# Mirrored image rows folded around the column transform, with plain fp32 matmuls in array halves

## Chip, cores and metric

One core of a Trainium2 chip runs the whole program in one launch. The metric is device time in microseconds (us), the median of several executions.

## What is computed

The reference is a network of a convolutional mixer, linear attention and a small feed-forward block on eight images of 56x56 positions with 256 channels. The change touches the mixer: a long two-dimensional convolution, done as a Fourier transform over image columns and rows, a product with the transform of a generated kernel, and the transform back. Cut to that part:

```python
xn = simple_rms(x)
u = jax.nn.silu(xn @ W_u.T + b_u)          # 8 x 56 x 56 x 512, the gate
v = jax.nn.silu(xn @ W_v.T + b_v)          # 8 x 56 x 56 x 512
g = rpe_coeffs(...)                        # 111 x 111 taps for each channel
y = irfft2(rfft2(v) * rfft2(g))[:56, :56]  # along both image axes, each channel by itself
out = (u * y) @ W_o.T + b_o + x
```

Everything is fp32. The kernel transforms with matmuls by cosine and sine matrices of 111 points, in place of a fast transform.

## The kernel before

The program runs its phases one after the other: `kernel_rows_phase` makes the taps and transforms them along rows; `project_phase` (names pr_) computes v and its row transform; `columns_phase` (co_) does the column transform, the product and the column transform back; `mix_phase` (mx_) does the row transform back, the gate and the output product; attention and feed-forward follow. Between phases the data lie in device memory (`v_rows`, `y_rows`). Each engine's program is an order written out by hand; engines meet at counting semaphores, and each queue (PE, DVE, ACT, POOL, and SP, which issues DMAs) is strictly in order.

**Project phase.** 56 chunks of 8 image rows, 4 tiles each (two image rows at partitions 0 to 55 and 64 to 119). For a chunk PE transposes x (L1064), projects four tiles (L135, three fp32r passes for each product), and makes the row transform of each tile as two fp32 matmuls, one for each half of the array's rows (L1084). DVE adds the bias (L1220), ACT applies silu (`gate`, L1142), and ACT and DVE copy the results out (L1148, L1228). POOL normalises x four chunks ahead (`normalise`, L1047 and L1051). SP, for chunk n, issues the load of x for chunk n+4 and then waits for chunk n's rows to store them: so the load for n+4 stands behind the store of chunk n-1.

**Column phase.** 56 frequencies (k), each with the spectrum of the taps and eight images (b). v is stacked to 112 partitions, its real and imaginary part. ACT and DVE split v and the taps into a high and a low fp32r part (L837, L882, L841, L887). PE makes, for an image, six fp32r matmuls forward (L135, `forward`) and two fp32 matmuls back (L806, L808, `inverse`), and twelve fp32r matmuls for the next frequency's spectrum. DVE multiplies with the spectrum (L902, L904), POOL adds the terms (L925, L928), and ACT copies the result (L862) and, in one go of three, the spectrum (L846). PE runs the inverse of an image two images behind its forward (`LAG = 2`); two PSUM slots hold forward results.

**Mix phase.** 56 chunks again: PE makes the row transform back (L1485) as two fp32 matmuls, one for each half of the array's columns, DVE multiplies it by the gate straight from PSUM (`mix`, L1710), PE turns and multiplies by W_o. POOL does two normalise and two residual operations for a chunk (L1429, L1433, L1442, L1445).

The order of a frequency on PE before:

```python
for b in range(LAG, BATCH):
    if b == BATCH // 2 + 1 and more:
        spectrum(k + 1)
    forward(k, b)
    inverse(k, b - LAG)
for b in range(LAG):
    if more:
        forward(k + 1, b)
    inverse(k, BATCH - LAG + b)
```

## Time and profile before

| | |
|---|---|
| median of three executions | 5406.36 us (5403.94 to 5410.94) |
| profiled execution, first to last instruction (span) | 5398.1 us |
| busy share of the span | PE 97%, PE's weight loads 68%, DVE 74%, ACT 47%, POOL 46% |
| project phase, 56 chunks | from about 677 to 1271 us |
| column phase, 56 frequencies | from about 1299 to 2847 us |
| mix phase, 56 chunks | from about 2858 to 3907 us |

The profiled execution's own device time is not listed apart from the three; 8.3 us of the median lie outside its span. In the timeline a row gives start and duration of one instruction or of several of the same kind in a row, and in brackets how long its engine had been idle and what released it. A matmul's duration holds its fill and drain, so the spacing of starts tells what it costs PE in a stream.

### The profile page before, as it was taken

What the parts mean: (1) busy time and instruction counts of PE and PEld (TensorE: products, weight loads), DVE (VectorE), ACT (ScalarE), POOL (GpSimd) and SP (SyncE); (2) the same over time, 40 slices, a digit from 0 to 9 for tenths busy, and PEclk for the clock granted to TensorE, in tenths of its full rate; (3) what the DMA queues carried; (4) which work ended last, traced back from release to release, by engine and by line L of the source; (5) the groups of instructions that cost most, each with busy time, mean ns of one, the idle gap of its engine ahead of it and who ended that gap; (6) DMA issues with size and microseconds to landing.
All of it is one profiled execution on the core that took longest, in us unless ns stands there. A gap on an engine that the chain in (4) does not pass through costs nothing. (4 is left out here: it accounts for less than half of the span.)

```text
span 5398.1 us, 89326 instructions
## 1 busy us (share of the span) xinstructions
PE 5214.1 (97%) x27048; PEld 3662.3 (68%) x27048; DVE 3997.7 (74%) x6176; ACT 2512.3 (47%) x4791; POOL 2489.9 (46%) x1381
## 2 busy tenths in 40 slices
PE   8999899997999999999998999999989999987999
PEld 6777655554555555555556777777767777765999
DVE  6777666666999999999996676766635666665887
ACT  5555577774434334343434555555532222211555
POOL 0000054443999999999995555555301111111332
PEclk9999999998999999999999999999999999998999
DMA  3222167775444444444446666666533333433443
GB/s 109 89 89 72 53 197 219 217 217 170 149 150 150 149 152 148 152 148 150 151 136 182 195 203 200 191 200 202 163 113 97 104 113 107 118 89 97 123 122 113
DMA packets 349121, 782.62 MB, mean 145 GB/s; under 512 B 43433, under 2 KB 147845, under 8 KB 339460
## 3 DMA queue, kind: packets, MB, share of 16 engines
q1 hardware_dynamic: 326596, 703.91, 44.2%
q10 hardware_dynamic: 22400, 77.08, 4.0%
q8 instruction: 73, 1.20, 0.1%
q14 instruction: 52, 0.43, 0.0%
HBM read 420.49 MB, written 360.38 MB: 145 GB/s over the span
## 5 line engine op out<-in xcount | busy, mean ns | idle before, releaser
L928 POOL TENSOR_TENSOR co_prod<-co_cross 111x512 f32<-111x512 f32 x448 | 848.8, 1895 | 0.0
L862 ACT ACTIVATE co_y_out<-co_y_ps 112x512 f32<-112x512 f32 x448 | 267.9, 598 | 928.2 <-PE co_y_ps L808 923.1
L925 POOL TENSOR_TENSOR co_prod<-co_direct 111x512 f32<-111x512 f32 x448 | 576.3, 1286 | 203.8 <-PE co_y_ps L808 116.0
L902 DVE TENSOR_TENSOR co_direct<-co_v_ps,co_spec 111x1024 f32<-111x1024 f32 x448 | 543.5, 1213 | 92.0 <-PE co_v_ps L135 87.9
L2012 POOL TENSOR_TENSOR at_t<-at_t,at_p_bias 112x1024 f32<-112x1024 f32 x56 | 137.7, 2470 | 889.3 <-DMA at_t<-t_tiles 889.3
L904 DVE TENSOR_TENSOR co_cross<-co_v_ps,co_spec 111x1024 f32<-111x1024 f32 x448 | 541.5, 1209 | 0.0
L135 PE MATMUL co_v_ps<-co_v_high,co_col_fwd_high 112*111 112x512 f32 x896 | 506.1, 565 | 1.4 <-DVE co_cross L904 1.4
L806 PE MATMUL co_y_ps<-co_prod,co_col_inv 111*112 111x512 f32 x896 | 458.2, 592 | 0.0
L808 PE MATMUL co_y_ps<-co_prod,co_col_inv 111*112 111x512 f32 x896 | 457.5, 592 | 0.1
L882 DVE TENSOR_TENSOR co_v_low<-co_v_in,co_v_high 112x1024 fp32r<-112x1024 f32 x224 | 372.3, 1662 | 0.0
L135 PE MATMUL co_v_ps<-co_v_low,co_col_fwd_high 112*111 112x512 f32 x896 | 354.3, 395 | 0.0
L2173 ACT ACTIVATE at_qk_t<-at_bank_ps 128x448 f32<-128x448 f32 x224 | 121.6, 543 | 499.1 <-PE at_bank_ps L135 499.1
L135 PE MATMUL co_v_ps<-co_v_high,co_col_fwd_low 112*111 112x512 f32 x896 | 349.1, 390 | 0.0
L1596 ACT ACTIVATE mx_mixed_high<-mx_turn_ps 128x448 fp32r<-128x448 f32 x224 | 121.8, 544 | 431.1 <-PE mx_turn_ps L1495 431.1
L808 PEld LDWEIGHTS co_y_ps<-co_prod,co_col_inv 111*112 111x112 f32 x896 | 156.0, 175 | 229.3 <-issue 212.3
L1220 DVE SCALAR_TENSOR_TENSOR pr_v_pre<-pr_v_ps,pr_inv,pr_v_bias 120x512 f32<-120x512 f32 x224 | 167.6, 748 | 150.8 <-PE pr_v_ps L135 145.5
L1442 POOL TENSOR_TENSOR mx_resid<-mx_x_in,mx_o_bias 112x1024 f32<-112x1024 f32 x56 | 134.0, 2393 | 311.2 <-DVE mx_t L1726 311.2
L306 POOL CAST kr_points<-kr_coords 6x448 fp32r<-6x448 f32 x28 | 15.2, 568 | 565.8 <-DMA kr_coords<-coords 565.8
L2502 POOL TENSOR_TENSOR ff_base<-ff_t,ff_n 112x1024 f32<-112x1024 f32 x56 | 132.7, 2370 | 301.3 <-DVE ff_out L2663 281.5
L1047 POOL TENSOR_TENSOR pr_gx<-pr_x_in,gn_rows 128x1024 f32<-128x1024 f32 x55 | 133.0, 2419 | 298.1 <-DMA pr_x_in<-x 298.1
L135 PE MATMUL mx_o_ps<-mx_w_o_high,mx_mixed_high 128*112 128x256 f32 x896 | 252.3, 282 | 3.5 <-DVE mx_mixed_low L1715 3.5
L135 PE MATMUL mx_o_ps<-mx_w_o_high,mx_mixed_low 128*112 128x256 f32 x896 | 252.2, 281 | 0.0
(277 smaller groups left out, 14268.5 us busy)
## 6 DMA issues: line engine op xcount, KB each, us to landing
v_rows<-pr_rows_out SPq DMA_DIRECT2D x56, 1792.0 KB, 8.2
co_v_in<-v_rows SPq DMA_DIRECT2D x448, 224.0 KB
y_rows<-co_y_out SPq DMA_DIRECT2D x448, 224.0 KB
mx_y_in<-y_rows SPq DMA_DIRECT2D x224, 448.0 KB, 5.5
kr_x_in<-x SPq DMA_DIRECT2D x56, 448.0 KB, 3.9
kern_rows<-kr_rows_out SPq DMA_DIRECT2D x28, 896.0 KB, 4.7
pr_x_in<-x SPq DMA_DIRECT2D x112, 224.0 KB
mx_x_in<-x SPq DMA_DIRECT2D x56, 448.0 KB, 5.3
```

What stands on the lines that cost most here:

```text
L135: last = nc.tensor.matmul(out, weights[a], data[b], start=start and i == 0, stop=stop and i == len(passes) - 1)
L806: nc.tensor.matmul(y_ps[b % 2][:2 * SIDE, :], col_inv[:, 0, :], prod[b % 2][:, :WIDE], start=True, stop=False)
L808: nc.tensor.matmul(y_ps[b % 2][:2 * SIDE, :], col_inv[:, 1, :], prod[b % 2][:, WIDE:], start=False, stop=True).then_inc(inv_mm, 1)
L862: nc.scalar.activation(y_out[:, b, :], y_ps[b % 2][:2 * SIDE, :], ACT.Copy).then_inc(y_ready, 1)
L882: nc.vector.tensor_tensor(v[1][:, images, :], v_in[:, images, :], v[0][:, images, :].bitcast(F32), ALU.subtract).then_inc(low_v, 1)
L902: nc.vector.tensor_tensor(direct[b % 2][:], v_ps[b % 2][:POINTS, :], spec[i][:, :2 * WIDE], ALU.mult).then_inc(real_terms, 1)
L904: nc.vector.tensor_tensor(cross[b % 2][:], v_ps[b % 2][:POINTS, :], spec[i][:, WIDE:], ALU.mult).then_inc(multiplied, 1)
L925: nc.gpsimd.tensor_tensor(prod[b % 2][:, :WIDE], direct[b % 2][:, :WIDE], direct[b % 2][:, WIDE:], ALU.subtract).then_inc(real_ready, 1)
L928: nc.gpsimd.tensor_tensor(prod[b % 2][:, WIDE:], cross[b % 2][:, :WIDE], cross[b % 2][:, WIDE:], ALU.add).then_inc(combined, 1)
L1220: nc.vector.scalar_tensor_tensor(out=v_pre[t % 2][:], in0=v_ps[t % 2][:SPAN, :], scalar=inv[:SPAN, j % GROUP * TILES + t:j % GROUP * TILES ...
L1442: nc.gpsimd.tensor_tensor(resid[u][:], x_in[u][:], o_bias[:].unsqueeze(1).to_broadcast(each), ALU.add).then_inc(resid_part, 1)
L2012: nc.gpsimd.tensor_tensor(t1[j % HELD][:], t1[j % HELD][:], p_bias[:].unsqueeze(1).to_broadcast([TILE, TILES, CH]), ALU.add).then_inc(t1_b ...
```

## The change

The image rows are stored in mirrored pairs (by the caller, outside the kernel, and put back there): each group of four is two rows and their mirror images. In the project phase POOL adds (`add_rows`) and DVE subtracts (`subtract_rows`) two tiles of silu results into `fold`, and the row transform takes `fold`. The even and odd parts that result make the column transform of an image real: two fp32 matmuls with 56 input rows each, in the two halves of the array's rows, and back two fp32 matmuls with 56 outputs each, in the two halves of its columns. No fp32r splits are left in the column phase. DVE writes all four terms of the product in one operation of 2048 elements; POOL adds them for six images of eight in one operation of 1024, and for images 2 and 6 PE adds them, with four matmuls. The inverse runs three images behind. The spectrum is four full fp32 matmuls, spread over four images, and its four copies on ACT are spread over images 4 to 7. In the mix phase ACT copies the odd part out of PSUM (`take_odd`), DVE unfolds (`unfold`), and POOL, in place of DVE, multiplies by the gate.

```diff
@@ columns_phase, PE
+                def spectrum(k, out, part):
...
+                    last = nc.tensor.matmul(taps_ps[:POINTS, bass.ts(out, WIDE)], col_taps[:, matrix, :], taps_in[:, part, :],
+                                            start=part == 0, stop=part == 1)
...
                 def forward(k, b):
                     n = k * BATCH + b
-                    pe.wait_ge(low_v, k * PAIRS + b // 2 + 1)
-                    buffer_free(pe, multiplied, n)
-                    for out in range(2):
-                        last = product(nc, v_ps[b % 2][:POINTS, bass.ts(out, WIDE)], [w[:, out, :] for w in col_fwd],
-                                       [x[:, b, :] for x in v], start=True, stop=True)
+                    pe.wait_ge(v_loaded[b // 2], k * 32 + 32)
+                    wait_slot(pe, multiplied, n)
+                    for part in range(2):
+                        side = slice(part * GAP, part * GAP + SIDE)
+                        last = nc.tensor.matmul(v_ps[b % 2][:POINTS, bass.ts(part, WIDE)], col_fwd[side, :], v_in[side, b, :],
+                                                start=True, stop=True)
...
+                    if b in SUMMED_BY_PE:
+                        pe.wait_ge(multiplied, SLOTS + n + 1)
+                        for term in range(2):
+                            for part in range(2):
+                                last = nc.tensor.matmul(y_ps[b % 2][part * GAP:part * GAP + SIDE, :],
+                                                        col_inv[:, part * SIDE:(part + 1) * SIDE],
+                                                        terms[b % RING][:, bass.ts(2 * part + term, WIDE)],
+                                                        start=term == 0, stop=term == 1)
...
                     for b in range(LAG, BATCH):
-                        if b == BATCH // 2 + 1 and more:
-                            spectrum(k + 1)
+                        if more and b > LAG:
+                            spectrum(k + 1, *divmod(b - LAG - 1, 2))
                         forward(k, b)
                         inverse(k, b - LAG)
@@ columns_phase, ACT (after the change; SUMMED_BY_PE = (2, 6), LAG = 3, TERMS = 4)
+                        if more and b >= TERMS:
+                            spectrum(k + 1, 1 - i, b - TERMS)
+                        wait_inverse(act, k, b)
...
+                    if col == TERMS - 1:
+                        last.then_inc(spec_ready, 1)
@@ columns_phase, DVE
                     dve.wait_ge(spec_ready, k + 1)
                     for b in range(BATCH):
...
+                        twice = [POINTS, 2, 2 * WIDE]
+                        nc.vector.tensor_tensor(terms[b % RING][:].rearrange("p (t n) -> p t n", t=2),
+                                                v_ps[b % 2][:POINTS, :].unsqueeze(1).to_broadcast(twice),
+                                                spec[i][:].rearrange("p (t n) -> p t n", t=2), ALU.mult).then_inc(multiplied, 1)
@@ project_phase, POOL
-                for n in range(1, GROUPS * GROUP):
-                    normalise(n // GROUP, n % GROUP)
+                def add_rows(s, j, pair):
+                    n = (s * GROUP + j) * PAIRS + pair
+                    done(pool, v_ready, 2 * n + 1)
+                    fold_free(pool, s, j, 2 * pair)
+                    nc.gpsimd.tensor_tensor(fold[2 * pair][:], v[2 * pair][:], v[2 * pair + 1][:], ALU.add).then_inc(sums_ready, 1)
...
+                for n in range(last + 1):
+                    add_rows(n // GROUP, n % GROUP, 1)
+                    if n + GROUP <= last:
+                        normalise((n + GROUP) // GROUP, n % GROUP)
+                    if n < last:
+                        add_rows((n + 1) // GROUP, (n + 1) % GROUP, 0)
@@ project_phase, PE
                 def row_pass(s, j, t):
                     n = (s * GROUP + j) * TILES + t
-                    done(pe, v_ready, n)
+                    pe.wait_ge(diffs_ready if t % 2 else sums_ready, (s * GROUP + j) * PAIRS + t // 2 + 1)
@@ mix_phase, POOL
+                for g in range(2 * PAIRS):
+                    mix(g, 0)
+                    mix(g, 1)
+                    if g + 2 < 2 * PAIRS:
+                        normalise((g + 2) // 2, g % 2)
+                    mix(g, 2)
+                    mix(g, 3)
+                    if g + 1 < 2 * PAIRS:
+                        residual((g + 1) // 2, (g + 1) % 2, first=g == 0)
@@ mix_phase, DVE
+                def unfold(s, u, pair):
+                    n = (s * 2 + u) * (TILES // 2) + pair
+                    dve.wait_ge(odd_ready, n + 1)
+                    for t, op in ((2 * pair, ALU.add), (2 * pair + 1, ALU.subtract)):
+                        once_past(dve, turned, (s * 2 + u - 1) * TILES + t + 1)
+                        nc.vector.tensor_tensor(gated[t][:], y_ps[0][:SPAN, :], odd[pair][:], op).then_inc(unfolded, 1)
```

Line numbers below are those of the changed kernel: L814 is the forward matmul, L832 and L825 the inverse (L825 where PE adds the terms), L803 the spectrum; L866 copies the spectrum and L878 a result on ACT; L1053, L1057 and L1063 are POOL's normalise and `add_rows`.

PE in the column phase, in the next to last frequency of the changed kernel, from the third piece of the next spectrum on:

```order
L803 MATMUL co_taps_ps<-co_taps_in,co_col_taps 111x512
L814 MATMUL co_v0_ps<-co_v_in,co_col_fwd 111x512 x2
L832 MATMUL co_y1_ps<-co_prod3,co_col_inv 56x512 x2
L803 MATMUL co_taps_ps<-co_taps_in,co_col_taps 111x512
L814 MATMUL co_v1_ps<-co_v_in,co_col_fwd 111x512 x2
L832 MATMUL co_y0_ps<-co_prod0,co_col_inv 56x512 x2
L814 MATMUL co_v0_ps<-co_v_in,co_col_fwd 111x512 x2
L832 MATMUL co_y1_ps<-co_prod1,co_col_inv 56x512 x2
L814 MATMUL co_v1_ps<-co_v_in,co_col_fwd 111x512 x2
L825 MATMUL co_y0_ps<-co_terms2,co_col_inv 56x512 x4
L814 MATMUL co_v0_ps<-co_v_in,co_col_fwd 111x512 x2
```

The seventh row is the forward matmul of the next frequency's image 0, the ninth that of its image 1, and the last that of its image 2; the tenth is the inverse of image 6. Between forward and inverse PE goes from row halves to column halves for every image, and the spectrum's pieces use the full array.

ACT in the same place, from image 3's copy of the result on:

```order
L878 ACTIVATE co_y_out<-co_y1_ps 120x512
L866 ACTIVATE co_spec1<-co_taps_ps 111x512
L878 ACTIVATE co_y_out<-co_y0_ps 120x512
L866 ACTIVATE co_spec1<-co_taps_ps 111x512
L878 ACTIVATE co_y_out<-co_y1_ps 120x512
L866 ACTIVATE co_spec1<-co_taps_ps 111x512
L878 ACTIVATE co_y_out<-co_y0_ps 120x512
L866 ACTIVATE co_spec1<-co_taps_ps 111x512
L878 ACTIVATE co_y_out<-co_y1_ps 120x512
```

The fourth copy of the spectrum, which releases the next frequency on DVE, now stands behind the result of image 6; before, three copies stood together ahead of the result of image 4.

POOL in the project phase, of the changed kernel, over one chunk and a half:

```order
L1053 TENSOR_TENSOR pr_gx0<-pr_x_in0,gn_rows 128x1024
L1057 TENSOR_TENSOR pr_gx0<-pr_gx0,gn_rows 128x1024
L1063 TENSOR_TENSOR pr_fold0<-pr_v0,pr_v1 120x512
L1063 TENSOR_TENSOR pr_fold2<-pr_v2,pr_v3 120x512
L1053 TENSOR_TENSOR pr_gx1<-pr_x_in1,gn_rows 128x1024
L1057 TENSOR_TENSOR pr_gx1<-pr_gx1,gn_rows 128x1024
L1063 TENSOR_TENSOR pr_fold0<-pr_v0,pr_v1 120x512
```

And before:

```order
L1047 TENSOR_TENSOR pr_gx0<-pr_x_in0,gn_rows 128x1024
L1051 TENSOR_TENSOR pr_gx0<-pr_gx0,gn_rows 128x1024
L1047 TENSOR_TENSOR pr_gx1<-pr_x_in1,gn_rows 128x1024
L1051 TENSOR_TENSOR pr_gx1<-pr_gx1,gn_rows 128x1024
L1047 TENSOR_TENSOR pr_gx2<-pr_x_in2,gn_rows 128x1024
```

The sum of tiles 0 and 1 of the next chunk, on which its first row transform waits, now stands behind the normalising of the chunk four ahead, which waits for the load of x. SP's order is as it was.

## Rows read from the trace of the kernel before

**Rows 1.** Windows: steady project, column, mix phase; length, busy: PE, PEld, DVE, ACT, POOL.

```profile
697.00:1267.00 570.00, 570.00 (x2605) 338.96 (x2603) 373.34 (x596) 450.18 (x1043) 244.85 (x103) 1.00 0.70 216
1326.00:2820.00 1494.00, 1494.00 (x4991) 870.84 (x4990) 1409.12 (x1140) 596.45 (x870) 1362.90 (x870) 1.00 0.49 149
2885.00:3890.00 1005.00, 1005.00 (x6496) 769.72 (x6495) 699.07 (x1459) 568.12 (x966) 513.57 (x216) 1.00 0.66 194
```

**Rows 2.** Timeline of PE in the column phase: start, duration, line.

```profile
2033.46 0.59 PE L806 MATMUL co_y_ps<-co_prod,co_col_inv 111*112 111x512 f32 x1
2033.89 1.02 PE L808 MATMUL co_y_ps<-co_prod,co_col_inv 111*112 111x512 f32 x2
2034.35 0.79 PE L135 MATMUL co_taps_ps<-co_taps_high,co_col_taps_high 111*111 111x512 f32 x1
2034.98 0.40 PE L135 MATMUL co_taps_ps<-co_taps_low,co_col_taps_high 111*111 111x512 f32 x1
2035.21 0.39 PE L135 MATMUL co_taps_ps<-co_taps_high,co_col_taps_low 111*111 111x512 f32 x1
...
2061.89 0.79 PE L135 MATMUL co_taps_ps<-co_taps_high,co_col_taps_high 111*111 111x512 f32 x1
```

**Rows 3.** Timeline of PE in the project phase, into and out of row halves.

```profile
1004.71 0.40 PE L135 MATMUL pr_v_ps<-pr_w_v_high,pr_x_t_low 128*120 128x512 f32 x1
1005.03 1.97 PE L1084 MATMUL pr_row_ps<-pr_v,pr_row_fwd 56*112 56x512 f32 x8
1006.94 0.50 PE L135 MATMUL pr_v_ps<-pr_w_v_high,pr_x_t_high 128*120 128x512 f32 x1
1007.27 0.39 PE L135 MATMUL pr_v_ps<-pr_w_v_low,pr_x_t_high 128*120 128x512 f32 x1
```

**Rows 4.** Timeline of PE in the mix phase, into and out of column halves.

```profile
3302.36 0.55 PE L1514 MATMUL mx_turn_ps<-mx_ident,mx_n 112*128 112x112 f32 x4
3302.84 1.93 PE L1485 MATMUL mx_y_ps<-mx_y_in,mx_row_inv 112*56 112x512 f32 x8
...
3305.03 0.39 PE L135 MATMUL mx_u_ps<-mx_w_u_low,mx_x_t_high 128*120 128x512 f32 x1
```

**Rows 5.** Timeline of DVE, then POOL, in the column phase.

```profile
2002.15 1.21 DVE L904 TENSOR_TENSOR co_cross<-co_v_ps,co_spec 111x1024 f32<-111x1024 f32 x1
2003.29 1.39 DVE L882 TENSOR_TENSOR co_v_low<-co_v_in,co_v_high 112x1024 fp32r<-112x1024 f32 x1
...
2003.54 2.29 POOL L928 TENSOR_TENSOR co_prod<-co_cross 111x512 f32<-111x512 f32 x1
...
2007.11 1.30 POOL L928 TENSOR_TENSOR co_prod<-co_cross 111x512 f32<-111x512 f32 x1
```

**Rows 6.** Timeline of ACT in the column phase; the first row follows PE L808.

```profile
2013.30 0.60 ACT L862 ACTIVATE co_y_out<-co_y_ps 112x512 f32<-112x512 f32 x1 [5.29 <-PE co_y_ps L808]
2013.79 1.56 ACT L846 ACTIVATE co_spec<-co_taps_ps 111x512 f32<-111x512 f32 x3
```

**Rows 7.** Attention phase: timeline of PE, then windows (third last column: clock).

```profile
3971.29 0.21 PE L2042 MATMUL at_bank_ps<-at_total_eps,at_row_head 128*32 128x1 f32 x5 [3.35 <-DVE at_sel L2255]
...
3972.00:3973.00 1.00, 1.00 (x9) 0.27 (x5) 0.00 (x0) 0.00 (x0) 0.00 (x0) 0.50 0.67 251
...
3975.00:3976.00 1.00, 1.00 (x12) 0.39 (x8) 0.00 (x0) 0.00 (x0) 0.04 (x1) 0.82 1.06 315
```

**Rows 8.** Timeline of SP, then POOL, then PE, in the project phase.

```profile
1012.96 0.36 SPq L1004 DMA_DIRECT2D v_rows<-pr_rows_out  x1
1013.58 2.09 SPq L999 DMA_DIRECT2D pr_x_in<-x  x2
...
1022.80 2.42 POOL L1047 TENSOR_TENSOR pr_gx<-pr_x_in,gn_rows 128x1024 f32<-128x1024 f32 x1 [5.49 <-DMA pr_x_in<-x]
1025.31 2.38 POOL L1051 TENSOR_TENSOR pr_gx<-pr_gx,gn_rows 128x1024 f32<-128x1024 f32 x1
...
1026.05 1.54 PE L1084 MATMUL pr_row_ps<-pr_v,pr_row_fwd 56*112 56x512 f32 x5
```

More of the change, by code:

```diff
@@ L60, in angles, with mirrored_rows, folded_slots @@
     return 2.0 * np.pi * ((np.outer(a, b) % POINTS) / POINTS)
+HALF_ROWS = CHUNK_ROWS // 2
+def mirrored_rows():
+    order = []
+    for first in range(0, SIDE // 2, 2):
+        order += [first, first + 1, SIDE - 1 - first, SIDE - 2 - first]
+    return np.array(order)
+def folded_slots():
+    place = np.arange(SIDE)
+    return place // CHUNK_ROWS * HALF_ROWS + place % HALF_ROWS, place % CHUNK_ROWS >= HALF_ROWS
 def shape_constants():
@@ L718, in pair_ahead, with wait_pooled, wait_inverse @@
-        def pair_ahead(k, b, more, ahead):
-            pair = b // 2 + ahead
-            if b % 2 == 0 and pair < PAIRS:
-                return k, pair
-            return (k + 1, pair - PAIRS) if b % 2 == 0 and more else None
+        def wait_pooled(eng, k, b):
+            if b >= 0:
+                eng.wait_ge(combined, (k + 1) * len(POOLED) + POOLED.index(b) + 1)
+            else:
+                eng.wait_ge(combined, k * len(POOLED) + POOLED.index(b + BATCH) + 1)
+        def wait_inverse(eng, k, b):
+            eng.wait_ge(inv_mm, (k + 1) * BATCH + b + 1)
@@ L821, in step @@
                         inverse(k, BATCH - LAG + b)
-                pe.sem_inc(inv_mm, SLOTS)
-                spectrum(0)
+                pe.sem_inc(inv_mm, BATCH)
+                pe.wait_ge(consts_in, 16 * len(loads))
+                for piece in range(4):
+                    spectrum(0, *divmod(piece, 2))
+                pe.wait_ge(y_clear, SLOTS)
                 for b in range(LAG):
@@ L868, in _ @@
-                split_taps(0)
-                for pair in range(HIGH_AHEAD):
-                    split_v(0, pair)
-                spectrum(0, 0)
+                for col in range(TERMS):
+                    spectrum(0, 0, col)
                 with act.Fori(0, LOOP) as s:
@@ L991, in columns, with slot, fold_free @@
             return slice(j % GROUP * TILES, (j % GROUP + width) * TILES)
+        PAIRS = TILES // 2
+        def slot(t, r):
+            return t % 2 * HALF_ROWS + t // 2 * 2 + r
+        def fold_free(eng, s, j, t):
+            if not (isinstance(s, int) and s == 0 and j == 0):
+                eng.wait_ge(row_mm, (s * GROUP + j - 1) * TILES + t + 1)
         with nc.Block() as block:
@@ L1083, in row_pass @@
                         side = slice(r * GAP, r * GAP + SIDE)
-                        last = nc.tensor.matmul(row_ps[t % 2][r][:ROWS, :], row_fwd[side, :], v[t][side, :], start=True, stop=True)
+                        last = nc.tensor.matmul(row_ps[t % 2][r][:ROWS, :], row_fwd[side, t % 2, :], fold[t][side, :],
+                                                start=True, stop=True)
                     last.then_inc(row_mm, 1)
@@ L1666, in step @@
                         store_t1(*before)
+                    if after:
+                        open_gate(*after, 1)
                     if later:
@@ L1776, in step @@
                     if now:
-                        low_part_mixed(*now, 0)
-                        mix(*now, 1)
+                        unfold(*now, 1)
+                        low_part_mixed(*now, 1)
+                    if before:
+                        residual(*before, 1)
                     if before2:
@@ L1782, in step @@
                         scale_gate(*after, 0)
-                    if before:
-                        residual(*before, 1)
                     if now:
-                        low_part_mixed(*now, 1)
-                        mix(*now, 2)
+                        low_part_mixed(*now, 2)
                     if before3:
                         take_norm(*before3)
-                    if after:
-                        scale_gate(*after, 1)
                     if before:
```

345 lines of the change are left out of this document (161 added, 184 removed).

## Prediction

> **What bounds the kernel now.** I first took the busy time of each engine over three steady stretches, since a total says nothing of stages [rows 1]. The first number after the length is PE's: it is busy for 570.0 us of 570, 1494.0 of 1494 and 1005.0 of 1005, at full clock. So in all three phases PE's own work sets the time, and the next engines are below it: in the column phase DVE with 1409 of 1494 and POOL with 1363. A change there pays only if it takes time from PE and no wait takes its place. Second, the timeline of PE, for the price of a matmul. In a stream an fp32 matmul of 512 columns comes as two passes whose starts lie 0.43 apart (2033.46, 2033.89), so 0.86 for one; an fp32r pass takes 0.23 (2034.98 to 2035.21) [rows 2]. A frequency lasts 2061.89 - 2034.35 = 27.54 us; 60 fp32r passes at 0.23 and 16 fp32 matmuls at 0.86 make 27.56. The model of PE closes. Third, the timelines of the other queues, for durations and for what each waits for.
>
> **Column phase: PE's work.** Two matmuls in opposite halves of the array already run side by side: eight passes in row halves issue in 1.7 us [rows 3], as do eight in column halves [rows 4], so four half matmuls cost what two full ones do. A frequency of the new kernel has 8 forward pairs, 6 inverse pairs, 2 images with two inverse pairs each, and 4 full matmuls of the spectrum: 22 x 0.86 = 18.9 us.
>
> Each change between full array and halves costs something. In the project phase the last full pass begins at 1004.71 and takes 0.23, the next full pass after the row halves ends its 0.23 before 1007.27; between lie 1007.04 - 1004.94 = 2.10 us for passes worth 4 x 0.43 = 1.71, so 0.39 for two changes [rows 3]. For column halves: four turns of 0.095 from 3302.36 end at 3302.74, the next full pass begins at 3305.03 - 0.23 = 3304.80, so 2.06 - 1.71 = 0.35 for two [rows 4]. I take 0.18 for one. The order has 20 changes in a frequency, 8 between full array and halves and 12 straight from row halves to column halves or back. No row shows a straight one. Its bounds are 0, if both halves count as one mode, and 0.37, if it is a way out and a way in; I take 0.18, nearest to both measured kinds. One change falls into the wait below, so 19 x 0.18 = 3.4 us.
>
> The Trainium skill, TensorEngine Tiling (Array Packing), section Tiling Modes, says that changing the tiling mode, and not just the tile, drains TensorE. By that rule, which speaks against this change, the straight changes are paid in full; without it they would be free and a frequency 12 x 0.18 = 2.2 us shorter, 121 us over the phase.
>
> **Column phase: a new wait.** At each frequency's start DVE's product for image 0 waits for the fourth copy of the spectrum. On ACT that copy stands behind the result of image 6, whose inverse on PE comes right before the forward of the next frequency's image 2; and this forward needs the slot that the product of image 0 frees. So from the issue's end of inverse 6: 0.16 until the last matmul is out (0.59 long, 0.43 apart [rows 2]), 0.49 for the result's copy and 0.60 for the spectrum's (0.60 long, next one 0.49 later [rows 6]), the product of 2048 elements, and four handovers of 0.04 to 0.05. A product of 1024 elements takes 1.21, and DVE's next operation starts 1.14 after it [rows 5], so one of 2048 takes at most 1.14 + 1.21 = 2.35 and, with one fixed part less, about 2.3. Sum: 3.7 us in which PE has nothing. DVE's 8 x 2.3 = 18.4 us and POOL's 6 x 2.4 = 14.4 (2.38 for 1024 elements [rows 8]) fit in the frequency, so nothing else waits. Frequency: 18.9 + 3.4 + 3.7 = 26.0 us.
>
> But such a gap moves the clock. After PE had stood idle for 3.35 us its granted clock went from 1.00 to 0.50 in the window at 3972, and the one at 3975 is back to 0.82 [rows 7]: some 3.4 us at 1.2 GHz in place of 2.4, so up to 1.7 us lost. The new gap is longer than that one. Part of the slow stretch falls on handovers, so I take 1.35: 27.4 us against 27.54, 56 x -0.14 = **-8 us**. The first frequency's preparation has no splits left, four of 512 elements at some 0.7 us (a little over half of 1.21): **-3**.
>
> **Project phase: the decisive part.** PE's matmuls stay the same in number and price. DVE gains two subtractions of 512 elements (some 0.7 each) on top of 373/570 x 10.51 = 6.9 us for a chunk, POOL two additions of 1.30 (a 512-element operation, the second POOL row of [rows 5]) on top of 4.9; neither fills 10.51 us. But the row transform now waits for POOL, and POOL's order puts normalise(n+4) ahead of the addition for tiles 0 and 1 of chunk n+1. Normalise waits for its x: the last rows show POOL idle 5.49 us before it, released by the DMA [rows 8]. SP, in an unchanged order, issues that load behind the store of chunk n-1. So a loop closes: the row transform of chunk n-1 begins at 1005.03 [rows 3], its rows are stored at 1012.96, the load goes out at 1013.58 and lands at 1022.80, 17.77 after the start; normalise ends 2.5 + 2.4 later, at 22.7; the addition takes 1.30 and some 0.15 to start, and only then can the row transform of chunk n+1 begin, at 24.1. Today it begins at 1026.05, 21.02 after 1005.03 [rows 8]. The loop spans two chunks: +3.1 us for two. It can be 0.5 worse: beside a DVE operation with two SBUF inputs (2003.29) POOL's operation took 2.29 instead of 1.30 [rows 5], and the new subtraction is one. So 1.55 to 1.8 us for a chunk, for the 52 chunks that have a chunk four ahead: 80 to 94, taken as **+87 us**. Below, the cost is 0, if the load lands earlier; above, the loop's idle time of about 1.7 us per chunk could pull the clock down (40 us more). I expect no fall: 1.7 is half of the gap that did it.
>
> The Trainium skill, GPSIMD Engine Reference, section Specifications, has this contention as GpSimd sharing its SBUF interfaces with VectorE, against DVE instructions with two SBUF inputs. The trace agrees: 2.29 and 1.30 us.
>
> **Mix phase and the rest.** A chunk takes 18.53 us. POOL was busy for 513.6/1005 x 18.53 = 9.5 of them and gets four operations of 1.30, 14.7 in all; ACT 10.5 and two copies of 0.60; DVE exchanges four multiplies for four adds [rows 1]. All stay beside PE, whose matmuls there do not change. Were the chain through POOL late, the output product would wait: 0 to +30 us; I take 0. Attention and feed-forward are unchanged.
>
> **The sum.** 87 - 8 - 3 = +76, and 3 more for clock falls now and then: +79. The profiled execution has a span of 5398.1, and with 8.3 us around it the median of 5406.36: 5398.1 + 8.3 + 79 = 5485.
>
> **Rivals.**
> A. The loop through POOL does not bind. It decides only if landing plus 4.9 + 1.45 us exceeds 21.02, so if x lands later than 14.7 us after the row transform; it lands at 17.77 today, but the load may find the DMA queues emptier once the pace slows. For it: the load takes 9.2 us, long for its size. Against: 3 us must vanish. Then 5406 - 8 - 3 = 5395. Chance 0.12. This is the case on the other side.
> B. The clock stays up in the column phase, since 3.7 us may come out shorter: 56 x (26.0 - 27.54) = -86 in place of -8: 5407. For it: the price of the 2048-element product is worked out, not seen, and the gap that did it was 3.35 us, not far below. Against: 3.35 us did. 0.14. With A as well: 5317, chance 0.04.
> C. Straight changes cost 0.30, or the clock is low twice in a frequency: 12 x 0.12 x 56 = +81 for the first, 1.0 to 1.7 a frequency for the second: 5541 to 5580, typically 5566. 0.12.
> D. The gaps of the project phase pull the clock down: +45, 5530. 0.06.
> E. The halves do not overlap here, so the change does not do what it says: 18 pairs x 0.86 x 56 = +867, 6350. 0.02. Against it: [rows 3, 4].
> The forecast: 0.50.
>
> **How the numbers follow.** A measurement of this kernel tells 0.2% (11 us) from no change. Faster by more: half of A, A with B, and B at its lucky end, 0.13. Within: the other half of A and part of B, 0.11. Slower: 0.76. The range takes in the forecast's own spread (mode changes of 0.15 or 0.21 move it by 19 x 0.03 x 56 = 32 us, the loop by 7, the mix phase by up to 30), A, B and most of C and D: 5392 to 5590.
>
> **What would show it.** Right: PE busy about 86% of the project phase, its row transforms released by POOL's addition, starts two chunks apart 24 us; in the column phase one gap of 3.5 to 3.9 us per frequency, before the forward of image 2 and released by DVE, behind it windows at clock 0.50, frequency 27.4 us; spacing from a forward pair to an inverse pair 0.86 + 0.18. Wrong: row transforms of the project phase 10.5 us apart; or the clock at 1.00 throughout the column phase; or many short gaps there, at every image, in place of one.

## The result, and the profile after

The changed kernel takes 5686.0 us (5682.3 to 5702.5) against 5405.2 for the kernel before: a ratio of 1.052, 95% interval 1.051 to 1.054. The direction was forecast, the size was not: +281 us in place of +79, and outside the range. In the profiled executions the difference of the spans, 5684.7 - 5398.1 = 286.6 us, lies as follows (each phase from PE's first to its last matmul):

| phase | before | after | difference | forecast |
|---|---|---|---|---|
| project | 593.7 | 742.3 | +148.6 | +87 |
| column | 1547.2 | 1570.2 | +23.0 | -11 |
| mix | 1058.9 | 1171.8 | +112.9 | 0 |
| all else | | | +2.1 | +3 |

The page of the kernel after, busy time by engine:

```profile
PE 5106.4 (90%) x26376; PEld 3085.8 (54%) x26376; DVE 3696.1 (65%) x5560; ACT 2330.9 (41%) x4677; POOL 2332.0 (41%) x1157
```

PE is busy for 108 us less than before, for 90% of the span in place of 97%. Matmuls at half clock count for longer in that sum; the column phase alone has some 290 us less work, as run e7 below shows. Windows of the kernel after: the first and the later part of the project phase, the column and the mix phase (length, busy us of PE, PEld, DVE, ACT, POOL; the third last column is the granted clock, the last but one the share of the DMA engines):

```profile
700.00:925.00 225.00, 196.81 (x871) 115.30 (x871) 162.48 (x238) 154.94 (x356) 142.38 (x74) 0.98 0.60 189
1000.00:1400.00 400.00, 334.91 (x1372) 190.37 (x1372) 274.43 (x375) 238.28 (x554) 229.64 (x114) 0.90 0.51 163
1470.00:2990.00 1520.00, 1317.69 (x4360) 302.41 (x4360) 987.68 (x436) 374.01 (x657) 765.79 (x326) 0.93 0.50 148
3050.00:4170.00 1120.00, 1035.97 (x6530) 763.14 (x6532) 701.85 (x1461) 617.67 (x1077) 789.96 (x437) 1.00 0.57 174
```

Where [rows 1] had PE busy all the time at clock 1.00, it is now busy for 87% and then 84% of the project phase, 87% of the column phase, and 92% of the mix phase. The clock is down in the first two, not in the third.

**Project phase.** The timeline of PE, SP, POOL and PE again, round the loop once, early in the phase:

```profile
888.12 1.97 PE L1105 MATMUL pr_row_ps<-pr_fold,pr_row_fwd 56*112 56x512 f32 x8 [1.38 <-POOL pr_fold L1063]
...
896.06 0.36 SPq L1010 DMA_DIRECT2D v_rows<-pr_rows_out  x1
896.68 2.12 SPq L1005 DMA_DIRECT2D pr_x_in<-x  x2
...
905.62 2.37 POOL L1053 TENSOR_TENSOR pr_gx<-pr_x_in,gn_rows 128x1024 f32<-128x1024 f32 x1 [2.98 <-DMA pr_x_in<-x]
908.07 2.81 POOL L1057 TENSOR_TENSOR pr_gx<-pr_gx,gn_rows 128x1024 f32<-128x1024 f32 x1
...
912.15 1.97 PE L1105 MATMUL pr_row_ps<-pr_fold,pr_row_fwd 56*112 56x512 f32 x8 [1.12 <-POOL pr_fold L1063]
```

This is the loop of the forecast: 888.12, store 7.94 later, load 0.62 after it, landed 8.94 after that (905.62), normalised by 910.88, added, and the row transform of two chunks on at 912.15: 24.03 us. For the loops that start between 815 and 925 us it is 24.0 to 24.5, with waits of 1.1 to 2.0 us on PE (one of 2.5 at 815). Before them the clock had fallen three times, in windows at 739, 767 and 790 us, at gaps of 2.0 to 2.8 us, and two chunks took 25.4 to 25.7. And later, in the timeline of PE and a window:

```profile
949.07 2.49 PE L1105 MATMUL pr_row_ps<-pr_fold,pr_row_fwd 56*112 56x512 f32 x8 [1.85 <-POOL pr_fold L1063]
...
951.00:952.00 1.00, 1.00 (x3) 0.47 (x2) 0.41 (x1) 0.63 (x3) 0.14 (x1) 0.50 0.71 251
```

After a gap of 1.85 us the clock went to one half. Gaps of 1.95 (before 852.11) and 1.97 (before 924.71) were no shorter, and behind them the clock stayed up: the next row transform came 4.87 us later, as always. From there on the loop runs at another length. The same rows, later in the phase, and the window after the first:

```profile
1032.31 3.65 PE L1105 MATMUL pr_row_ps<-pr_fold,pr_row_fwd 56*112 56x512 f32 x8 [4.11 <-POOL pr_fold L1063]
...
1044.31 0.35 SPq L1010 DMA_DIRECT2D v_rows<-pr_rows_out  x1
...
1054.22 2.38 POOL L1053 TENSOR_TENSOR pr_gx<-pr_x_in,gn_rows 128x1024 f32<-128x1024 f32 x1 [4.86 <-DMA pr_x_in<-x]
...
1060.30 1.20 PE L1105 MATMUL pr_row_ps<-pr_fold,pr_row_fwd 56*112 56x512 f32 x2 [4.47 <-POOL pr_fold L1063]
```

```profile
1033.00:1034.00 1.00, 1.00 (x4) 0.31 (x2) 0.00 (x0) 0.00 (x0) 0.48 (x1) 0.50 0.55 186
```

The gap is now 3.6 to 4.6 us at every second chunk. Behind it the clock is 0.50 and the row transform takes 3.65 in place of 1.97, so the chunk's second row transform comes 6.56 us after the first in place of 4.86: 1.7 us late. The store comes 12.0 us after the first row transform in place of 7.94, so another 2.4 us are lost behind the second one. These are DVE's, as its timeline and POOL's show in the same loop:

```profile
1037.79 2.34 DVE L1225 TENSOR_SCALAR pr_guarded<-pr_root 128x8 f32<-128x8 f32 x1
...
1041.98 1.28 DVE L1252 COPY pr_rows_out<-pr_row_ps 112x512 f32<-112x512 f32 x2
...
1037.40 2.70 POOL L1057 TENSOR_TENSOR pr_gx<-pr_gx,gn_rows 128x1024 f32<-128x1024 f32 x1
```

DVE's operation on eight columns (L1225) takes 0.17 us in the loop of 24 us (at 903.66, with nothing of POOL beside it). Here it starts 0.39 us after POOL's second normalise, lasts 2.34 and ends with it, and so in all 15 loops between 980 and 1376 us (2.33 to 2.37). DVE's copies of the rows stand behind it in its queue, and ACT's behind a silu that waits for DVE; the last ends at 1044.11. The load goes out so much later, and the next gap is as long again: 24.0 + 1.7 + 2.4 = 28.1, measured 1060.30 - 1032.31 = 27.99 us. The long gap keeps itself alive, through the clock, through DVE's place beside POOL, and through the queue of SP.

**Column phase.** PE, then ACT and DVE, at the start of a frequency, and two windows:

```profile
2212.04 1.11 PE L814 MATMUL co_v_ps<-co_v_in,co_col_fwd 56*111 56x512 f32 x4 [3.69 <-DVE co_terms L903]
2213.09 1.77 PE L832 MATMUL co_y_ps<-co_prod,co_col_inv 111*56 111x512 f32 x4
...
2208.40 0.60 ACT L878 ACTIVATE co_y_out<-co_y_ps 120x512 f32<-120x512 f32 x1 [1.82 <-PE co_y_ps L825]
2208.89 0.59 ACT L866 ACTIVATE co_spec<-co_taps_ps 111x512 f32<-111x512 f32 x1
...
2209.69 6.69 DVE L903 TENSOR_TENSOR co_terms<-co_v_ps,co_spec 111x2048 f32<-111x2048 f32 x3 [4.87 <-ACT co_spec L866]
```

```profile
2212.00:2213.00 1.00, 0.96 (x4) 0.27 (x4) 1.00 (x1) 0.00 (x0) 0.84 (x1) 1.00 0.21 76
2214.00:2215.00 1.00, 1.00 (x5) 0.22 (x4) 1.00 (x2) 0.10 (x1) 1.00 (x2) 0.50 0.19 74
```

The one gap, 3.69 us, released by DVE's product, which the fourth copy of the spectrum (2208.89) released. Behind it the clock is at one half for some 3.4 us, in every fifth frequency or so for twice as long. A forward pair and the change after it cost 2213.09 - 2212.04 = 1.05, still at full clock: 0.86 + 0.19.

**Mix phase.** ACT, then DVE, POOL and PE, in one chunk:

```profile
3412.27 1.28 ACT L1638 ACT_TABLE_LOAD   x1 [1.51 <-DVE mx_u_pre L1759]
...
3414.10 0.58 ACT L1644 ACTIVATE mx_odd<-mx_y_ps 120x512 f32<-120x512 f32 x1
...
3414.80 1.29 DVE L1767 TENSOR_TENSOR mx_gated<-mx_y_ps,mx_odd 120x512 f32<-120x512 f32 x2 [1.97 <-ACT mx_odd L1644]
...
3420.93 0.61 DVE L1813 COPY mx_n_t<-mx_turn_ps 128x448 f32<-128x448 f32 x1
...
3415.57 2.53 POOL L1492 TENSOR_TENSOR mx_gated<-mx_gated,mx_gate 120x512 f32<-120x512 f32 x2 [1.89 <-DVE mx_gated L1767]
...
3416.99 0.62 PE L1544 MATMUL mx_turn_ps<-mx_ident,mx_gated 120*128 120x120 f32 x4 [0.35 <-POOL mx_gated L1492]
...
3421.69 0.60 PE L1512 MATMUL mx_turn_ps<-mx_ident,mx_gx 112*128 112x112 f32 x4 [1.27 <-DVE mx_n_t L1813]
```

The odd part of tiles 2 and 3 was in PSUM at about 3411.0, after PE's L1534. ACT takes it at 3414.10, because the gate of tile 3 is before it in its queue: that one waits for DVE until 3412.27, and then loads a table for 1.28 us. Unfold (3414.80), POOL's multiply (3415.57) and what DVE has queued behind unfold, down to its copy at 3420.93, are late, and PE waits twice: 0.35 and 1.27 us. A chunk takes 20.6 us in place of 18.53; these two waits are 1.6 of the 2.1 us, and where the rest lies was not followed.

### The profile page after: what moved, and what is told of

It reads as the page before. It is cut to its first block and busy times, and to the rows that moved or that the text cites. A ratio compares the mean times of both kernels' runs of the same rounds, so it can differ in the third digit from the quotient of the medians.

```text
span 5684.7 us, 86662 instructions
## 1 busy us (share of the span) xinstructions
PE 5106.4 (90%) x26376; PEld 3085.8 (54%) x26376; DVE 3696.1 (65%) x5560; ACT 2330.9 (41%) x4677; POOL 2332.0 (41%) x1157
## 5 line engine op out<-in xcount | busy, mean ns | idle before, releaser
L903 DVE TENSOR_TENSOR co_terms<-co_v_ps,co_spec 111x2048 f32<-111x2048 f32 x448 | 1017.6, 2289 | 562.6 <-ACT co_spec L866 290.4
L921 POOL TENSOR_TENSOR co_prod<-co_terms 111x1024 f32<-111x1024 f32 x336 | 789.2, 2356 | 806.1 <-DVE co_terms L903 806.0
L878 ACT ACTIVATE co_y_out<-co_y_ps 120x512 f32<-120x512 f32 x448 | 267.5, 597 | 1157.7 <-PE co_y_ps L832 869.7
L814 PE MATMUL co_v_ps<-co_v_in,co_col_fwd 56*111 56x512 f32 x1792 | 555.8, 700 | 206.7 <-DVE co_terms L903 206.7
L814 PEld LDWEIGHTS co_v_ps<-co_v_in,co_col_fwd 56*111 56x111 f32 x1792 | 133.0, 185 | 609.3 <-DVE co_terms L903 367.5
L1492 POOL TENSOR_TENSOR mx_gated<-mx_gated,mx_gate 120x512 f32<-120x512 f32 x224 | 283.6, 1287 | 327.3 <-DVE mx_gated L1767 327.3
L832 PE MATMUL co_y_ps<-co_prod,co_col_inv 111*56 111x512 f32 x1344 | 410.4, 693 | 1.4 <-POOL co_prod L921 1.4
L1105 PE MATMUL pr_row_ps<-pr_fold,pr_row_fwd 56*112 56x512 f32 x896 | 250.3, 681 | 103.1 <-POOL pr_fold L1063 102.7
L803 PE MATMUL co_taps_ps<-co_taps_in,co_col_taps 111*111 111x512 f32 x448 | 252.0, 646 | 25.4 <-DMA co_col_inv<-col_inv 24.3
L155 PE MATMUL mx_o_ps<-mx_w_o_low,mx_mixed_high 128*112 128x256 f32 x896 | 252.0, 281 | 0.0
L2127 PE MATMUL at_bank_ps<-at_keys,at_n_tok 112*128 112x256 f32 x896 | 233.1, 384 | 6.6 <-DVE at_keys L2379 5.3
L832 PEld LDWEIGHTS co_y_ps<-co_prod,co_col_inv 111*56 111x56 f32 x1344 | 67.1, 139 | 306.8 <-issue 299.1
L1063 POOL TENSOR_TENSOR pr_fold<-pr_v 120x512 f32<-120x512 f32 x112 | 170.4, 1528 | 130.7 <-ACT pr_v L1167 125.9
```

Source lines behind the costliest of these rows:

```text
L155: last = nc.tensor.matmul(out, weights[a], data[b], start=start and i == 0, stop=stop and i == len(passes) - 1)
L803: last = nc.tensor.matmul(taps_ps[:POINTS, bass.ts(out, WIDE)], col_taps[:, matrix, :], taps_in[:, part, :], start=part == 0, stop=part == 1)
L814: last = nc.tensor.matmul(v_ps[b % 2][:POINTS, bass.ts(part, WIDE)], col_fwd[side, :], v_in[side, b, :], start=True, stop=True)
L832: last = nc.tensor.matmul(y_ps[b % 2][part * GAP:part * GAP + SIDE, :], col_inv[:, part * SIDE:(part + 1) * SIDE], prod[b % RING][:, bass. ...
L878: nc.scalar.activation(y_out[:, b, :], y_ps[b % 2][:SPAN, :], ACT.Copy).then_inc(y_ready, 1)
L903: nc.vector.tensor_tensor(terms[b % RING][:].rearrange("p (t n) -> p t n", t=2), v_ps[b % 2][:POINTS, :].unsqueeze(1).to_broadcast(twice), ...
```

## Experiments

Each edit stands on the changed kernel, where nothing else is said. The ratio is to the kernel before, timed beside it. Times are medians; the phases are those of one profiled execution, which for e2 took 5590 us against a median of 5609.5.

| run | time, us | ratio (95%) | project | column | mix |
|---|---|---|---|---|---|
| changed kernel | 5686.0 | 1.052 (1.051 to 1.054) | 742 | 1570 | 1172 |
| e1 additions first | 5557.5 | 1.027 (1.025 to 1.029) | 617 | 1567 | 1168 |
| e5 load early | 5566.3 | 1.029 (1.027 to 1.031) | 626 | 1565 | 1172 |
| e2 odd part first | 5609.5 | 1.038 (1.036 to 1.041) | 723 | 1566 | 1092 |
| e3 spectrum early | 5818.9 | 1.077 (1.075 to 1.079) | 726 | 1714 | 1172 |
| e7 and taps twice | 5377.4 | 0.995 (0.994 to 0.997) | 762 | 1256 | 1166 |
| e8 all cures | 5173.8 | 0.957 (0.956 to 0.959) | 617 | 1257 | 1097 |
| e9 and no sums on PE | 5094.3 | 0.942 (0.941 to 0.944) | 618 | 1181 | 1096 |
| e10 filler, project | 5618.4 | 1.039 (1.037 to 1.041) | 684 | 1565 | 1172 |
| e11 filler, column | 5630.6 | 1.041 (1.040 to 1.043) | 740 | 1526 | 1168 |

Where the project phase is not touched it takes 723 to 762 us: its loop falls into one length or another (25.5 to 27.3 us for two chunks all along in e2).

**e1: the additions first.**

```diff
-                    if n + GROUP <= last:
-                        normalise((n + GROUP) // GROUP, n % GROUP)
                     if n < last:
                         add_rows((n + 1) // GROUP, (n + 1) % GROUP, 0)
+                    if n + GROUP <= last:
+                        normalise((n + GROUP) // GROUP, n % GROUP)
```

> Edit: in the project phase POOL adds tiles 0 and 1 of chunk n+1 before it normalises chunk n+4. Theory (the addition stands behind a normalise that waits for x, in a loop through SP's store and load; the idle time of the loop bunches at every second chunk, 4.5 us at a time, and pulls the clock down, which lengthens the loop further): project phase back from 742 us to 594 to 605 us, POOL's addition never behind a DMA wait, clock 1.00 there, whole program 5686 - 140 = 5540 to 5550. Rival (the additions are late by themselves, or slowed beside DVE's subtraction with two SBUF inputs): the phase stays above 650 us, whole program above 5600.

Measured: 5557.5, project phase 617 us, clock 1.00 throughout. Waits of the project phase, us in total, times, longest, first of the changed kernel:

```profile
POOL pr_gx L1053 <- DMA pr_x_in<-x: 161.4, 51, 5.0
...
PE pr_row_ps L1105 <- POOL pr_fold L1063: 101.8, 48, 4.6
```

and of e1:

```profile
PE pr_row_ps L1105 <- POOL pr_fold L1063: 19.9, 27, 1.4
...
POOL pr_gx L1053 <- DMA pr_x_in<-x: 9.6, 25, 0.6
```

The loop is gone, with it 125 of the 149 us. What was expected too low is the rest: every second chunk PE still waits, as rows of PE's and POOL's timelines in e1 show, 21.83 us apart where it was 21.02.

```profile
1002.13 1.97 PE L1105 MATMUL pr_row_ps<-pr_fold,pr_row_fwd 56*112 56x512 f32 x8 [0.71 <-POOL pr_fold L1063]
...
1023.96 1.97 PE L1105 MATMUL pr_row_ps<-pr_fold,pr_row_fwd 56*112 56x512 f32 x8 [0.71 <-POOL pr_fold L1063]
...
1022.17 1.74 POOL L1063 TENSOR_TENSOR pr_fold<-pr_v 120x512 f32<-120x512 f32 x1
```

That is 0.8 us for two chunks, 23 us in the phase. It is now the second row transform of a chunk that waits, for the sum of tiles 2 and 3, which stands directly behind the normalise (1017.37 to 1022.17) and takes 1.74 us in place of 1.27: a short queue on POOL where before there was the load. The rival, additions late by themselves, holds for this rest and not for the loop.

**e5: the load early.** The same loop, cut at SP. The main lines of the edit; one load ahead of the loop and the loop's new bounds are left out:

```diff
...
                 def step(s, j, left):
-                    if left >= GROUP:
-                        sp.wait_ge(gx_ready, s * GROUP + j + 1)
-                        load(s + 1, j)
+                    if left > GROUP + 1:
+                        sp.wait_ge(gx_ready, s * GROUP + j + 2)
+                        load(s + 1 + (j + 1) // GROUP, (j + 1) % GROUP)
```

> Edit: POOL's order as changed, but SP issues the load of x for a chunk one step (one chunk's store) earlier. Theory of the loop: landing moves some 10.5 us ahead, so normalise no longer waits for the DMA and the project phase falls to 594 to 610 us, whole program 5540 to 5560, as with the other cure. Rival (POOL's order itself is too tight, 4.9 us of normalising between two additions): the phase stays above 640 us.

Measured: 5566.3, project phase 626. POOL's wait for the load has left the list, and PE's wait reads

```profile
PE pr_row_ps L1111 <- POOL pr_fold L1069: 24.6, 29, 1.4
```

So either end of the loop cures it, and POOL's order alone was no fault. The phase is again 16 to 32 us longer than expected: POOL's sums still come late by up to 1.4 us at a time.

**e2: the odd part first.**

```diff
                         take_mixed(*now, 0)
-                        open_gate(*now, 3)
                         take_odd(*now, 1)
+                        open_gate(*now, 3)
```

> Edit: in the mix phase ACT takes the odd part of tiles 2 and 3 out of PSUM before it opens the gate of tile 3. Theory (the odd part stood behind a gate that waits for DVE and then loads a table of 1.28 us, so unfold, POOL's mix, the norm's shift and the turn of x on PE all come 1.3 us or more late): PE's waits of 0.35 and 1.27 us in each chunk go, a chunk takes 18.6 to 19.0 us in place of 20.6, mix phase 1172 down to 1060 to 1085, whole program 5585 to 5600. Rival (POOL's multiply, 1.28 us where DVE took 0.68, is what makes the chain long): a chunk stays above 20 us, whole program above 5650.

Measured: 5609.5, mix phase 1092, 79 us less; a chunk takes 19.1 us. The program's time is 10 us and the phase 7 us above what was expected: both of PE's waits should have gone. ACT and PE:

```profile
3400.27 0.60 ACT L1644 ACTIVATE mx_odd<-mx_y_ps 120x512 f32<-120x512 f32 x1 [0.39 <-PE mx_y_ps L1534]
3401.38 1.28 ACT L1638 ACT_TABLE_LOAD   x1 [0.51 <-DVE mx_u_pre L1759]
...
3409.28 0.60 PE L1512 MATMUL mx_turn_ps<-mx_ident,mx_gx 112*128 112x112 f32 x4 [0.31 <-DVE mx_n_t L1813]
```

The odd part is taken as soon as PE has it, and of PE's two waits 0.31 is left. POOL's multiply still takes 1.28 us, so its duration was not what made a chunk 20.6 us. A chunk stays 0.6 above 18.53, over the phase the 34 us that are left; that last wait is half of it, and neither what holds DVE's copy back there nor the other half was followed.

**e3: the spectrum early.**

```diff
-                        if more and b >= TERMS:
-                            spectrum(k + 1, 1 - i, b - TERMS)
+                        if more and b in (4, 5):
+                            spectrum(k + 1, 1 - i, 2 * (b - 4))
+                            spectrum(k + 1, 1 - i, 2 * (b - 4) + 1)
```

> Edit: in the column phase ACT copies the spectrum two pieces at a time, ahead of the results of images 4 and 5, in place of one ahead of each of images 4 to 7. Theory (one wait of 3.8 us per frequency through that fourth copy, and the clock fall it causes): the gap goes, the clock is 1.00 throughout, a frequency takes 22 pairs x 0.86 + 20 mode changes x 0.18 = 22.5 us, the phase 1570 down to 1265 to 1290, whole program 5385 to 5410. Rival (mode changes, POOL's additions or DVE's products bound it right behind): a frequency stays above 24.5 us, whole program above 5500.

Measured: 5818.9, slower than the changed kernel by 133 us. The theory missed by over 400 us; the rival's time (above 5500) came, but from none of the causes that it names. PE's wait for DVE was gone, but in its list of waits there is

```profile
PE co_taps_ps L803 <- DMA co_taps_in<-kern_rows: 278.2, 50, 6.1
```

some 5.6 us in each frequency, and the clock at one half behind it for some 6.8 us. There is one buffer for the taps, and SP issues their load for frequency k+2 behind the store of images 4 and 5 of frequency k. In the steady column phase of the changed kernel PE waits for the taps only twice, 1.1 us in all: while it stands before the third forward, they come in. Half of the theory held (that wait can be removed), the half that nothing else binds did not.

**e7: e3, and a second buffer for the taps.** SP's part of the edit; the second buffer and its semaphores are left out:

```diff
...
+                        if more2 and pair == 0:
+                            sp.wait_ge(taps_mm, k + 1)
+                            load_taps(sp, k, 2, i)
                         if more and pair + 1 < PAIRS:
                             next_v(k, 1, pair + 1)
                         if more2 and pair + 1 == PAIRS:
-                            sp.wait_ge(taps_mm, k + 2)
-                            load_taps(sp, k, 2)
                             next_v(k, 2, 0)
```

> Edit: the spectrum's copies two at a time as in the run before, and a second buffer for the taps, so that their load for frequency k+2 goes out at the start of frequency k. Theory (with the spectrum's copies early, PE stood 6 us per frequency at the spectrum for the load of the taps, issued behind the store of images 4 and 5; nothing else binds): both gaps are gone, a frequency takes 22.5 to 23.0 us, column phase 1265 to 1300, whole program 5385 to 5420. Rival (the loads of v, which have one buffer, or POOL, are next behind the taps): a frequency stays at 24 us or more, column phase above 1340.

Measured: 5377.4, column phase 1256. The window over its steady part:

```profile
1470.00:2690.00 1220.00, 1217.71 (x4362) 288.96 (x4362) 988.09 (x438) 371.10 (x651) 774.09 (x329) 1.00 0.62 184
```

PE is busy for 1217.7 of 1220 us at full clock. A steady frequency takes 22.27 us (first product to first product on DVE): 18.9 for the pairs and 3.35 for 20 mode changes, 0.17 each. Rows of PE, one step of each kind but one:

```profile
1911.85 1.11 PE L804 MATMUL co_taps_ps<-co_taps_in,co_col_taps 111*111 111x512 f32 x2
1912.89 1.11 PE L815 MATMUL co_v_ps<-co_v_in,co_col_fwd 56*111 56x512 f32 x4
1913.93 1.07 PE L833 MATMUL co_y_ps<-co_prod,co_col_inv 111*56 111x512 f32 x4
1914.93 1.11 PE L815 MATMUL co_v_ps<-co_v_in,co_col_fwd 56*111 56x512 f32 x4
```

From the full array to row halves, and from row halves straight to column halves, starts lie 1.04 apart; from column halves straight to row halves 1.00, and to the full array 1.01 (1903.80 to 1904.81). With 0.86 for the work a change costs 0.18, and 0.14 out of column halves. The phase of 1256 us is the price of the changed column phase with nothing in its way, 291 us less than before. With this alone the kernel is faster than before by 0.5% (0.3 to 0.6), although project and mix phase are as slow as they were.

**e8, e9: all cures, and no sums on PE.** e8 is e7 with e1 and e2. e9 further sets `SUMMED_BY_PE = ()`, so POOL adds the terms of all eight images.

> Edit: the previous one with the additions first on POOL in the project phase and the odd part first on ACT in the mix phase. If the three phases are independent, the gains add: 5686 - 129 (project) - 77 (mix) - 290 (column) = 5190, 5170 to 5215, faster than the kernel before by 190 us or more. If they are not, or if the column phase is held by something else, 5220 to 5350.

> Edit: all cures except the taps' second buffer being the only column edit: in addition POOL adds the terms of all eight images and PE of none. If PE sets the frequency (22.5 us with two images summed by PE), it loses two pairs of 0.86 and a frequency takes 20.8 us, 95 us less than with all cures, 5090 to 5110. If POOL sets it (8 additions of 2.36 and their waits, 18.9 busy, plus handovers) or DVE (18.4), a frequency stays between 21 and 23 us, 5110 to 5210; the two images on PE are then worth nothing or something.

Measured: 5173.8 and 5094.3. The phases are independent: e8's are those of e1, e7 and e2 to within 5 us. In e9 the window over the steady column phase is

```profile
1340.00:2460.00 1120.00, 1111.00 (x3870) 257.03 (x3870) 968.77 (x430) 368.15 (x646) 1003.99 (x429) 1.00 0.66 197
```

POOL is busy for 1004 and DVE for 969 of 1120 us, and PE still for 1111. The column phase is 76 us shorter than in e8, where two pairs of 0.86 would give 96. The 20 us of difference were not followed; the waits of PE's weight loads for POOL's sums, 0.8 us at most, may be part of them. A frequency of 20.76 and 20.95 us in turn is the one that was expected with PE setting the pace. So the two images that PE adds are not worth their matmuls once POOL's additions fit behind PE.

**e10, e11: the waits stay, the clock is held up.** Both add products whose results nothing reads, inside a wait of PE. In the project phase, ahead of the wait for the first sum:

```diff
-                    pe.wait_ge(diffs_ready if t % 2 else sums_ready, (s * GROUP + j) * PAIRS + t // 2 + 1)
                     buffer_free(pe, row0_out, n)
                     buffer_free(pe, row1_out, n)
+                    if t == 0:
+                        nc.tensor.matmul(row_ps[0][0][:ROWS, :], row_fwd[:SIDE, 0, :], v_bias[:SIDE, :], start=True, stop=True)
+                    pe.wait_ge(diffs_ready if t % 2 else sums_ready, (s * GROUP + j) * PAIRS + t // 2 + 1)
```

> Edit: the changed kernel as it is; in the project phase PE issues one idle matmul of 56 rows (0.86 us, its result is overwritten by the row transform behind it) before it waits for a chunk's first sum. The wait itself stays. Theory (the loop alone gives 24.1 to 24.5 us for two chunks, as in the first twenty chunks; what turned it into 28 is that a gap of 1.9 us pulled the clock to 1.2 GHz, which made the rows, their store and the next load late): with gaps under 1.2 us the clock stays up, two chunks take 24.1 to 24.5 us throughout, project phase 742 down to 675 to 690, whole program 5620 to 5635, although PE has 48 us more to do. Rival (the 28 us come from POOL's and DVE's contention or from the table load, not from the clock): two chunks stay at 26 to 28 us, whole program 5670 or more.

Measured: 5618.4, project phase 684. PE's timeline (the second row transform, L1107, of two chunks that lie two apart) and the window over the phase:

```profile
1000.88 1.97 PE L1107 MATMUL pr_row_ps<-pr_fold,pr_row_fwd 56*112 56x512 f32 x8
...
1024.93 1.54 PE L1107 MATMUL pr_row_ps<-pr_fold,pr_row_fwd 56*112 56x512 f32 x6
```

```profile
690.00:1300.00 610.00, 584.66 (x2508) 327.16 (x2506) 432.67 (x653) 424.57 (x978) 390.89 (x203) 1.00 0.59 187
```

From 1000.88 to 1024.93 two chunks take 24.05 us, at clock 1.00. With 48 us more work on PE the phase is 58 us shorter. 684 - 594 = +90 is the forecast's term of 87, so the loop was sized rightly. The other 58 us come with the fall of the clock, but not all by the clock: in the slow loops 1.7 of the 4.1 us are slow matmuls and 2.4 are DVE's operation held beside POOL, and in e10 that one takes 0.17 us throughout. The run does not part the two, since with the gap filled neither appears; the rival that puts the 28 us down to POOL and DVE was wrong as to what starts it and right for a part of its size.

In the column phase, ahead of the frequency's third forward:

```diff
+                            if b == LAG - 1:
+                                wait_slot(pe, y_ready, k * BATCH + BATCH - 1)
+                                for _ in range(3):
+                                    nc.tensor.matmul(y_ps[1][:SIDE, :], col_inv[:, :SIDE], spec[i][:, :WIDE],
+                                                     start=True, stop=True)
                             forward(k + 1, b)
```

> Edit: the changed kernel as it is; in the column phase PE issues three idle matmuls of 56 columns (2.6 us, overwritten by the inverse behind them) in the wait of 3.7 us before each frequency's third forward. The wait itself stays. Theory (the wait gives 26.0 us for a frequency, the clock fall behind it the other 1.6): a gap of about 1.1 us is left, clock 1.00, a frequency takes 26.0 to 26.2 us, column phase 1570 down to 1470 to 1485, whole program 5595 to 5610. Rival (the mode changes and pairs are dearer than counted, the clock costs little): a frequency stays at 27 us or more, whole program above 5650.

Measured: 5630.6, column phase 1526: the time lies between theory and rival, and a frequency of 27.1 us in the median is the rival's. Its rows of PE tell why, and the window gives the clock:

```profile
2003.11 1.11 PE L803 MATMUL co_taps_ps<-co_taps_in,co_col_taps 111*111 111x512 f32 x2 [0.83 <-DMA co_taps_in<-kern_rows]
...
2025.04 1.11 PE L814 MATMUL co_v_ps<-co_v_in,co_col_fwd 56*111 56x512 f32 x4 [1.12 <-DVE co_terms L908]
...
2030.01 1.11 PE L803 MATMUL co_taps_ps<-co_taps_in,co_col_taps 111*111 111x512 f32 x2 [0.65 <-DMA co_taps_in<-kern_rows]
```

```profile
1480.00:2900.00 1420.00, 1309.74 (x4498) 317.25 (x4496) 947.41 (x420) 356.50 (x626) 738.59 (x315) 1.00 0.51 152
```

The gap before the forward is 1.12 us and the clock 1.00. But from 2003.11 to 2030.01 a frequency takes 26.9 us, and in it stands a wait for the taps of 0.65 to 0.83 us before the spectrum. It is the wait of e3, which shows as soon as the frequency is shorter; the list of waits has 53 of them, 46.5 us in all. Take 0.9 off the 27.1, and 26.2 is left, the 26.0 of the forecast.

## Why the prediction was right or wrong

- *Price of a pair, and of a change of mode (22 x 0.86 and 0.18 each).* Right: e7's frequency of 22.27 us is 18.9 + 3.35, 0.17 for a change. The straight changes between row halves and column halves cost 0.18 one way and 0.14 the other, near the value taken, and neither of its bounds. The Trainium skill, TensorEngine Tiling (Array Packing), section Tiling Modes, says that a change of tiling mode drains TensorE; the trace agrees in so far as a straight change is paid for, with the spacings of 1.04 and 1.00 us in e7.
- *The new wait of 3.7 us through ACT's fourth copy.* Right in place, cause and size: 3.69.
- *The clock falls behind it, 1.35 us lost.* Right in kind, small in size. 27.64 - 26.0 = 1.6 in most frequencies, and 3 in the eleven where the clock stays down twice as long or more, for which the sum had no term. Terms: -8 and -3 forecast, +23 measured.
- *Project phase, +87.* The loop was right step by step (7.9, 0.6, 9.0, 5.2, 1.3: 24.0 to 24.5 us) and e10 gives it +90. Wrong was the sentence "I expect no fall: 1.7 is half of the gap that did it". The gaps are uneven, 1.1 to 2.8 us; one of 2.0 did it first, and one of 1.85 started the long stretch of slow loops. That price stood in rival D as +45, added once; the fall is fed back through store and load and brings DVE's operation beside POOL's, which the forecast did not have, and all this made 58 in the profiled execution.
- *Mix phase, 0.* Wrong, and the largest error, 113 us. The step was to compare busy times (POOL 14.7 of 18.53 us and so on) and to conclude that everything stays beside PE. The new copy on ACT was priced at 0.60, its place in ACT's queue not at all: behind a gate that waits for DVE and then loads a table. One place further up in that queue it costs 79 us less (e2); the cause of the other 34 stays open. The diff and the order of ACT told this, and the chain was never laid out as it was for the other two phases. The "0 to +30" put a delay down to the chain through POOL; it came from ACT's queue, ahead of POOL.
- *The range.* It had C at up to 5580 and D at 5530 as alternatives, not as terms that add, and no case for the mix phase above +30. The 8.3 us put outside the span were mostly the spread between executions (in each run listed some 2 us lie outside); nothing hangs on it, as the sum adds them back to the median.

## What to carry to other kernels

A step added to an in-order queue costs what stands ahead of it, not its own duration: lay out the chain with the waits of its neighbours in the queue, at every engine the change touches, also where busy times leave room. When a wait is removed, look for what was hidden in it before counting the gain (here the load of the taps, 5.6 us behind a wait of 3.7). And an idle gap that may lower TensorE's clock, inside a loop that passes through that engine, is priced round the loop, not once; a shift of 2 us can also bring together operations of two other engines that had missed each other before.

## What the runs showed of the hardware

Gaps of 1.85 and 2.03 us on TensorE, in a loop where it was else busy, were followed by the clock of 1.2 GHz; gaps of 1.95, 1.97 and 2.54 us in the same phase were not. All the gaps of 3.7 us in the column phase were. A stretch at 1.2 GHz lasted some 3.4 us in most cases and twice that in every fifth frequency or so of the column phase. Matmuls of no use in the gap kept the clock at 2.4 GHz: 48 us of them, off the path, made the project phase 58 us shorter (e10). A change of the array's mode cost 0.18 us, and 0.14 out of column halves, also straight from one kind of half to the other (e7). An operation of VectorE on eight columns, 0.17 us by itself, lasted 2.34 us when it started beside a GpSimd operation of 1024 elements and 1.28 beside one of 512, and ended within 0.05 us of it each time, 19 times in the project phase of the changed kernel.
